# A deformable convolution, one attention block and a 256-step cell on one core: order of the group stage, banks and rings of the first tile, fills

## What is computed

```python
x = x + deformable_conv(group_norm(x))       # 3x3, 9 taps, learned offsets and masks, bilinear samples
t = tokens(x)                                # 4 images x 256 tokens x 64 channels
t = t + attention(layer_norm(t))             # 8 heads of 32, softmax, projection, gated GELU, two norms
t = t + cell(layer_norm(t))                  # 256 sequential steps, 64 states, 4 images side by side
...
def step(carry, xs):
    i_t = sigmoid(xi_t + h @ V_i); g_t = tanh(xg_t + h @ V_c); o_t = sigmoid(xo_t + h @ V_o)
    c_new = h * c + i_t * g_t
    h_new = o_t * tanh(c_new)
```

## Time and profile before

| | us |
|---|---|
| median of 3 runs | 384.69 |
| all three runs | 384.69, 386.04, 384.68 |
| the profiled execution, its own time | 385.77 |
| its span, first to last instruction | 384.0 |
| PE busy | 364.0 (95%) |
| DVE busy | 239.1 (62%) |
| ACT busy | 225.2 (59%) |
| POOL busy | 56.5 (15%) |

### The profile page before, as it was taken

The page is one execution under the profiler, slowest core; times in us unless marked ns, Lnnn a source line. Parts: engine busy times, 40 slices in busy tenths (PEclk is TensorE's granted clock), DMA queues, the critical chain, the costliest instruction groups (busy, mean ns, idle before and its releaser), DMA issues.

```text
span 384.0 us, 15270 instructions
## 1 busy us (share of the span) xinstructions
PE 364.0 (95%) x5880; PEld 194.9 (51%) x5880; DVE 239.1 (62%) x1234; ACT 225.2 (59%) x1073; POOL 56.5 (15%) x124
## 2 busy tenths in 40 slices
PE   8999999899999999999999999999999999999996
PEld 2576765454554455445645554554455455543332
DVE  3388665645656666666666666757675666664443
ACT  2496664615854785477548655864686478544342
POOL 3101001311211220122011211211121112110000
PEclk9999999999999999999999999999999999999999
DMA  8000000000000000000000000000000000000000
GB/s 253 15 2 5 12 15 15 14 2 3 3 4 3 7 3 2 3 7 4 3 3 5 5 2 5 4 4 3 5 4 3 3 7 3 3 2 6 3 2 4
DMA packets 4806, 4.33 MB, mean 11 GB/s; under 512 B 3837, under 2 KB 4286, under 8 KB 4734
## 3 DMA queue, kind: packets, MB, share of 16 engines
q1 hardware_dynamic: 4432, 2.84, 2.7%
q10 hardware_dynamic: 302, 0.52, 0.4%
HBM read 2.57 MB, written 0.26 MB: 7 GB/s over the span
## 4 chain that ended last, share of the span: by engine, by line
PE 67%; DVE 15%; ACT 11%; issue 6%; DMA 1%; DVEq 0%; ACTq 0%
PE bank L758 18%; PE bank L394 12%; PE bank L546 9%; DVE bank L1290 6%; PE bank L563 5%; DVE H L1300 5%; ACT bank L934 4%; ACT bank L927 4%; PE bank L461 4%; PE bank L584 4%; PE bank L451 3%; PE bank L422 2%; ACT E L859 2%; PE bank L655 1%; PE bank L689 1%
## 5 line engine op out<-in xcount | busy, mean ns | idle before, releaser
L394 PE MATMUL bank<-FB 128*128 128x512 bf16 (+3 forms) x490 | 141.1, 369 | 1.2 <-DVE FB L956 1.2
L758 PEld LDWEIGHTS bank<-H,VW 64*32 64x32 f32 x3060 | 52.1, 106 | 104.9 <-DVE H L1300 103.1
L927 ACT ACTIVATE bank<-bank 64x8 f32<-64x8 f32 x256 | 37.6, 147 | 87.8 <-PE bank L758 84.6
L758 PE MATMUL bank<-H,VW 64*32 64x4 f32 x3060 | 74.3, 176 | 11.9 <-DVE H L1300 1.5
L1290 DVE TENSOR_TENSOR_SCAN bank<-bank,SU 64x12 f32<-64x12 f32 x256 | 48.5, 189 | 49.9 <-ACT bank L927 47.3
L1300 DVE SCALAR_TENSOR_TENSOR H<-TO,bank 64x4 f32<-64x4 f32 x256 | 40.7, 159 | 44.8 <-ACT bank L934 34.1
L394 PEld LDWEIGHTS bank<-FB 128*128 128x128 bf16 x490 | 38.7, 99 | 22.1 <-issue 4.2
L371 POOL TENSOR_SCALAR E<-E,rinv 128x256 f32<-128x256 f32 x62 | 29.8, 480 | 126.1 <-DVE rinv L1092 126.1
L934 ACT ACTIVATE bank<-bank 64x4 f32<-64x4 f32 x256 | 38.4, 150 | 15.9
L931 ACT ACTIVATE TO<-bank 64x4 f32<-64x4 f32 x256 | 43.8, 171 | 6.3
L1284 DVE SCALAR_TENSOR_TENSOR SU<-H,bank 64x4 f32<-64x4 f32 x256 | 41.2, 161 | 9.1
(11 more groups left out here) (123 smaller groups left out, 311.1 us busy)
## 6 DMA issues: line engine op xcount, KB each, us to landing
AW<-in_attn_w SPq DMA_DIRECT2D x1, 768.5 KB, 8.2
DW<-in_dcn_w SPq DMA_DIRECT2D x1, 576.0 KB, 6.7
X<-in_x_fm SPq DMA_DIRECT2D x1, 256.0 KB, 3.3
X<-in_x_fm ACTq DMA_DIRECT2D x1, 256.0 KB, 5.5
T<-T0T SPq DMA_DIRECT2D x16, 16.0 KB, 1.8
Y<-YT SPq DMA_DIRECT2D x16, 16.0 KB, 1.8
out_dram<-OUT SPq DMA_DIRECT2D x8, 32.0 KB, 1.4
CW<-in_conv_w SPq DMA_DIRECT2D x1, 243.5 KB, 4.0
```

Source lines behind the costliest of these rows:

```text
L394: nc.tensor.matmul(idle[:, 0:n], FB[:, 0:P], FB[:, 0:n], start=True, stop=True)
L758: mm = nc.tensor.matmul(gate_out(m, gate, r, slice(B * s, B * (s + 1))), VW[0:C, gate, r], H[0:C, (STEPS * m + s - 1) % RING, :], start=Fa ...
L927: nc.scalar.activation(GT[:, :, 1:3].rearrange("p b g -> p g b"), b_cell[m % 2][0:C, 0:2 * P].rearrange("p (g s b) -> p g s b", g=2, b=B)[ ...
```

## The change

Five edits. (1) `COLS_GROUPS` falls from 4096 to 3072 columns. (2) In the group loop, `keys_queries` moves from the end of iterations 5 and 8 to iterations 6 and 9, behind `tokens` and ahead of the gathers; `channels` and `values` move behind the gathers of their iterations; ACT's `keys_out` follows to iterations 6 and 9; DVE's `first_queries(b)` moves from the first group of iterations 7 and 10 (g = 21, 30) to that of iterations 8 and 11 (g = 24, 33). (3) The turned probabilities of units 5, 6 and 7 get a bank each (`b_et_last`), ET becomes a ring of four, and the turns and weighings of units 4 to 7 are written in another order. (4) O is copied by image pairs: images 0 and 1 from one bank, images 2 and 3 from another. (5) At offset 28 of tile 0 the fill is 512 columns instead of 1536, and one of two fills in the last turns is gone.

```diff
@@
-KEYS_AT = (4, 7, 10)
+KEYS_AT = (6, 9)
@@
-COLS_GROUPS = 4096
+COLS_GROUPS = 3072
@@
-        ET = sb("ET", [P, 2, HALVES, P])
+        ET = sb("ET", [P, UNIT_RING, HALVES, P])
@@
+        b_et_last = {5: b_s1, 6: b_c1, 7: b_s0}
@@ def turned_bank(m, u)
-            return (b_et if m else b_s1 if u in (5, 7) else b_et_first)[:, 0:N]
+            return (b_et if m else b_et_last.get(u, b_et_first))[:, 0:N]
@@ def turn_probs(m, u)
                 elif m == 0 and i >= 5:
-                    pe.wait_ge(et_sb, i - 1)
-                    pe.wait_ge(e_inv, 4)
+                    pe.wait_ge(e_inv, i - 1)
@@ def weigh(m, u)
-                dst = b_pv if m else b_pv_last if b == B - 1 else b_pv_first
-                if m == 0 and u == NU - HG:
-                    pe.wait_ge(e_inv, NU - HG)
+                dst = b_pv if m else b_pv_last if b >= B // 2 else b_pv_first
+                if m == 0 and u == NU // 2:
+                    pe.wait_ge(e_inv, 3)
@@ TensorE's loop over iterations j
                 if j in TOKENS_AT:
                     tokens(TOKENS_AT.index(j))
+                if j in KEYS_AT:
+                    keys_queries(KEYS_AT.index(j))
+                if j >= 1:
+                    for g in range(BATCH * (j - 1), BATCH * j):
+                        gather(g)
                 if j in CHANNELS_AT[:-1]:
                     channels(CHANNELS_AT.index(j))
                 if j in VALUES_AT:
                     values(VALUES_AT.index(j))
-                if j >= 1:
-                    for g in range(BATCH * (j - 1), BATCH * j):
-                        gather(g)
-                if j - 1 in KEYS_AT[:-1]:
-                    keys_queries(KEYS_AT.index(j - 1))
@@ TensorE, last turns of tile 0
-            for u in range(4, NU):
-                if u >= NU - 2:
-                    fill(COLS_EARLY, b_x)
-                turn_probs(0, u)
-                weigh(0, u - 1)
-            weigh(0, NU - 1)
+            turn_probs(0, 4)
+            weigh(0, 3)
+            pe.wait_ge(e_inv, 5)
+            fill(COLS_EARLY, b_et_last[6])
+            turn_probs(0, 5)
+            turn_probs(0, 6)
+            weigh(0, 4)
+            turn_probs(0, 7)
+            weigh(0, 5)
+            weigh(0, 6)
+            weigh(0, 7)
@@ TensorE's loop over steps
-                    fill(COLS_EARLY if g < start(0) + NARROWED or g == start(0) + CELL_INPUT - 1 else MOST, b_cell[1])
+                    fill(COLS_EARLY if g < start(0) + NARROWED or g >= start(0) + CELL_INPUT - 2 else MOST, b_cell[1])
@@ ACT, turned(m, u)
-                if i >= 2:
-                    act.wait_ge(pv_mm, i - 1)
+                if i >= UNIT_RING:
+                    act.wait_ge(pv_mm, i - UNIT_RING + 1)
@@ ACT's loop over groups
+                    if j in KEYS_AT:
+                        keys_out(KEYS_AT.index(j))
                     if j in VALUES_AT:
                         values_out(VALUES_AT.index(j))
-                    if j - 1 in KEYS_AT[:-1]:
-                        keys_out(KEYS_AT.index(j - 1))
@@ DVE's loop over groups
-                if last == 0 and j - 3 in TOKENS_AT:
-                    first_queries(TOKENS_AT.index(j - 3))
+                if last == 0 and j - 2 in KEYS_AT:
+                    first_queries(KEYS_AT.index(j - 2))
@@ DVE, copies to O
-            for hg in range(HG):
-                heads_early(hg)
-            heads_last()
+            heads_of(slice(0, B // 2), b_pv_first, NU // 2).then_inc(o_early, 1)
+            heads_of(slice(B // 2, B), b_pv_last, NU).then_inc(o_done, HG)
```

More of the change, by code:

```diff
@@ L584, in weigh @@
                         mm = nc.tensor.matmul(dst[r, P * hg + TT * b:P * hg + TT * (b + 1)],
-                                              V[:, b, half, c], ET[:, i % 2, half, TT * h:TT * (h + 1)],
+                                              V[:, b, half, c], ET[:, i % UNIT_RING, half, TT * h:TT * (h + 1)],
                                               start=(half == 0), stop=(half == HALVES - 1), skip_group_check=True)
@@ L640, in project_turned @@
                 if m == 0:
-                    pe.wait_ge(o_early, HG)
+                    pe.wait_ge(o_early, 1)
                 if hg == 0 and m >= 1:
@@ L864, in turned @@
                 act.wait_ge(et_mm, i + 1)
-                if i >= 2:
-                    act.wait_ge(pv_mm, i - 1)
-                nc.scalar.copy(ET[:, i % 2, :, :].rearrange("p h q -> p (h q)"), turned_bank(m, u)
+                if i >= UNIT_RING:
+                    act.wait_ge(pv_mm, i - UNIT_RING + 1)
+                nc.scalar.copy(ET[:, i % UNIT_RING, :, :].rearrange("p h q -> p (h q)"), turned_bank(m, u)
                                ).then_inc(et_sb, 1)
@@ L1118, in _, with heads_of @@
                     token_norm(TOKENS_AT.index(j - 2))
-                if last == 0 and j - 3 in TOKENS_AT:
-                    first_queries(TOKENS_AT.index(j - 3))
[L1122 to L1133, removed]
+                if last == 0 and j - 2 in KEYS_AT:
+                    first_queries(KEYS_AT.index(j - 2))
+            def heads_of(images, src, units):
+                dve.wait_ge(pv_mm, units)
+                return nc.vector.tensor_copy(O[:, :, :, images],
+                                             src[:, 0:HG * P].rearrange("p (g b t) -> p g t b", g=HG, b=B)[:, :, :, images])
             token_norm(2)
```

## The result

The changed kernel is slower: the ratio of its runs to those of the kernel before is 1.0082, with a 95% interval of 1.0043 to 1.0121. The runs behind it are 388.16 and 389.05 us, against five of before between 384.68 and 386.04. The median over all five runs of the changed kernel is 403.45 us, because in three of them, the profiled one among them (403.75 us, mean granted clock 0.945), TensorE's clock also lay at its lower level for long stretches, and the ratio leaves these out. The profile is therefore compared with that of before only where its granted clock is 1.00.

The account below looks back on a forecast made before the run. The recurrence takes most time but stays unchanged; TensorE bounds the group stage, where the change is mainly decided. Against the median, 384.69 + 4.32 - 0.79 - 0.29 = 387.93, so 387.9 us, range 386.1 to 389.5.

Parts of the forecast that it names:

- The new wait: Group stage: TensorE stands in `values` for KF copies behind late queries, 2.64 us for each of two images, +5.28 us.
- A to QS: Group stage, DVE: one A ahead of the scaled queries, a link in the chain from the gathers, 0.64 us.
- The wait removed: Group stage: turning normalised tokens behind the gathers ends TensorE's wait on YT, 0.48 us for each of two images, -0.96 us.
- The last probabilities: First tile: last turn, weighings and O copy end earlier, -0.79 us, with ends 0 and -0.95.
- Fills at offset 28: First tile: fewer fills ahead of the input let LN's turn start sooner, -0.29 us, ends 0 and -0.48.
- The head: Ahead of the convolution: two fills fewer, -0.43 us against the profiled run, 0 against the median.
- The recurrence costs the same: Recurrence loop, 293.56 us: the diff touches nothing on it, so no change to its 1.14 us step.
- the faster one: DVE's queue, groups 21 to 24: queries written before sampling make both waits vanish, 382.65 us; chance 0.08.
- the loss is given back later: Stage after the group stage: TensorE's 1.69 us of idle time absorbs part of the loss, 386.24 us; chance 0.07.
- A clock that falls in the stops: Group stage: stops lower TensorE's clock, 0 to 5.8 us more for two, 390.8 us; chance 0.04.
- the rival that has all of it at the lower level: Head: the whole convolution stays at the lower clock level, +3.2 us, 391.1 us; chance 0.03.

Follow-up runs that it names:

- Experiments 1: Changed kernel with DVE scaling the queries of images 0 and 1 ahead of the sampling instead of behind it: 382.86 us, ratio 0.9946 to the kernel before.
- experiment 2: Kernel before with only the group stage's new order; banks, ring, O and fills as before: 390.0 us, ratio 1.0122.
- experiment 3: Changed kernel with ten 512-column fills ahead of the values of images 0 and 1: 389.16 us, ratio 1.0103 to the kernel before.
- experiment 4: Kernel before with the group stage's new order, but the queries scaled ahead of the sampling: 383.32 us, ratio 0.9966.
- 7: Changed kernel with queries ahead of the sampling and one tiny DVE memset more ahead of the last sampling: 383.2 us, ratio 0.994 to the kernel before.
- 11: Changed kernel with queries ahead of the sampling, a spare DVE memset, and both places of fills put back as before: 382.48 us, ratio 0.9941 to the kernel before.
- experiment 9: Kernel before with 3072 instead of 4096 columns of fill ahead of the convolution: 384.68 us, ratio 0.9992.
- 5: Kernel before with only the first tile's edits (banks, ring of four ET, order, one fill fewer there, O by image pairs): 384.41 us, ratio 0.9994.
- Experiment 8: Kernel before with the two early O copies put together into one, so DVE's program is one instruction shorter: 384.71 us, ratio 1.0.

## Why the prediction was right

The forecast was 387.9 us, 0.8% above the kernel before; measured is 0.82%. Step by step:

- **The new wait** was the step that decided, and it held: 4.08 us from the gathers' start forecast, 44.39 - 40.25 = 4.14 measured; 5.28 us for the two waits forecast, 5.3 measured. The link that was short is A to QS, 0.64 forecast from the mean of two A, 43.32 - 42.61 = 0.71 measured. Experiments 1, 2 and 3 exclude the other readings.
- **The wait removed** was mis-sized: 0.96 us for two images, where experiment 4 gives about 1.2 and its trace 0.63 for each. The step behind L480 also starts 0.2 us sooner where it is a batch of turns; why it does isn't shown.
- **The last probabilities**: -0.79 forecast, -0.84 measured to the end of O. The copy of 128 elements took 0.29 us, not 0.39 as its like-sized one in the recurrence.
- **Fills at offset 28**: -0.29 forecast, 7.54 - 7.25 = -0.29 measured.
- **The head**: 0 for the median was right, and for its reason. The runs of before lie in two groups, 384.3 to 384.9 and 385.7 to 386.3 us; the execution of the rows, 385.77 us, with fills at the lower level up to 9.67, is of the second. The same holds in the other experiments: the profiled executions of 4, 7 and 11, which are of the later group of their kernels, have the second fills 0.43 us apart throughout, and those of the earlier group have them at the upper level (eight in 1.89 or six in 1.46 us). For the later group -0.43 was forecast; experiment 9's runs show about -0.5, and in experiment 7's profile the step behind the convolution starts 14.12 - 13.68 = 0.44 us sooner than in that of before, 0.13 of it by an earlier XN.
- **"The recurrence costs the same"** is the one step that failed, by 0.65 us in experiments 1 and 5 and by 293.64 - 292.85 = 0.79 in experiment 3, which is the changed kernel but for the fills in its stops. My argument covered waits between engines; it didn't cover DVE's own stops.

The terms as measured, -1.2 + 5.3 - 0.84 - 0.29 + 0.65, give +3.6 us, 0.9%: inside the interval. Experiment 3's trace bears out the sum without the recurrence: from the start of the convolution to the first new state it takes 90.47 - 8.67 = 81.80 us, before 88.50 - 9.67 = 78.83, so +2.97. Two of the misses, 0.25 us of gain and 0.65 us of loss, partly cancel, so the forecast is nearer than its terms; that much was luck.

Of the rivals, the faster one (the queries ahead of the sampling) is experiment 1: 382.65 forecast for it, 382.86 measured, and the sign turns at the point named. That the loss is given back later didn't happen (experiment 2). A clock that falls in the stops was seen once, behind the second stop of the profiled execution, and cost 2.87 us, where that rival allowed up to 2.9 for a stop. The ratio doesn't hold it: its two runs have a granted clock of 1.000 and 0.998 as a whole, and experiment 2 has the same stops and the whole loss at 1.000. The convolution ran at the upper level in experiment 9 and lost 0.6 us to a late rise in experiment 7, so the rival that has all of it at the lower level didn't happen either. The Trainium skill (TensorE: Matmul & The Clock Gate, Part 1) has activity release the clock; the trace agrees, with fills of 0.43 us in the head giving way to fills of about 0.24 us (1.46 / 6).

## What to carry to other kernels

When a step is moved on one engine, write down what stands ahead of it in that engine's own program, and what that in turn waits for: here the place of one DVE step, behind the sampling and an A, tied the keys to gathers that they don't use. A chain of short rows of the trace of before, added link by link from start to start, sized a wait that didn't exist yet to within 0.1 us. And measure the parts of a bundle alone: this one holds 2 us of gain and a loss over twice as large.

## What I had not expected of the hardware

DVE has stops of about 0.2 to 0.3 us with no named cause, at steps that repeat between kernels: experiments 1, 3 and 5, whose DVE programs are one computing instruction shorter, have them on the same steps of the recurrence (57, 112 and 150 most of all), and a memset of one column at the end of the group stage, long before those steps, removes them (293.50 to 292.93 us). Experiment 8 shows that the count of computing instructions isn't the whole rule; what is stays open.
